# Turning a graph network's row tiles for TensorE: identity products and ScalarE copies, or transposing transfers

## The chip, the core and the metric

The kernel runs on one core of one Trainium2 chip. A core has a matrix engine (TensorE, in the profile PE, with its weight loads as PEld), VectorE (DVE), ScalarE (ACT), GpSimd (POOL) and SyncE (SP), which run side by side and meet at semaphores, and 16 DMA engines that move data between memories. ScalarE and SyncE each have a queue on which they issue transfers. The metric is the time of one execution on the device in microseconds (us); less is better.

## The reference

A graph with 1,250 nodes, 512 features and 21,250 directed edges goes through four residual layers, each followed by a layer norm over the features:

```python
x = layernorm(x + gcn(x))      # normalised adjacency, batch norm over nodes, gelu
x = layernorm(x + sage(x))     # two layers relu(h @ W_self + mean(h[src]) @ W_neigh + b)
x = layernorm(x + rgcn(x))     # two relations; w[r] = sum_b att[r,b] * basis[b], a sigmoid gate per node
x = layernorm(x + gin(x))      # relu((h + sum(h[src])) @ W1 + b1) @ W2 + b2
```

Each layer is made of products of the node matrix (1,250 x 512) with 512x512 weights, and of sums over a node's edges, which the kernel does as products with a dense count matrix.

## The kernel before

The nodes are ten tiles of 128 rows (`NT = 10`). After a first stage that counts the edges into `A` and `AT` and mixes the first basis matrices, the work goes through seven units, `UNITS`, numbered 0 to 6, with 1, 2, 2, 3, 3, 1 and 1 weight matrices. A unit has two phases:

- **dense**: for each tile `t`, `dense(t, j)` multiplies the tile of the input with each weight matrix. Numbers are kept as a sum of two float16 parts (high and low), so a product of a tile and a matrix is 12 matmuls of 128x128 by 128x512 (line 635). The bank pair is `j = t % 2`. ScalarE then takes the high part of the result out of PSUM (`z_out`, line 911), VectorE the low part (`z_low`, line 1265) and, where a unit has one, the node's own term (line 1273). `dense(t)` waits until that is done for tile `t - 2`.
- **aggregation**: for each tile, `agg(t, j)` sums over the neighbours (line 669, 20 matmuls per tile, 40 with two relations). VectorE and ScalarE turn the sum into the next unit's input: `after_agg` (line 1325), `ln_step` or `relu_step` for the high part in `S16`, `low_part` (lines 1280 and 1283) for the low one, which raises `s_ready`. Unit 0 aggregates in turned form (line 694), followed by the batch norm and `back` (line 704), and unit 6 has only the dense phase (`last_tile`, line 1352).

TensorE contracts over partitions, so a tile of `S16` (128 nodes x 1,024: high and low part) has to be turned before `dense(t)`. Before the change `turn(t, j)` does that: eight products of a 128x128 block with the identity `ident` into the PSUM tile `T` (line 609), and then ScalarE copies `T` into `hT[:, j]` in `hT_out` (line 855). `T` exists once and `hT` twice, so a tile is turned while TensorE works on the one before it, and `hT_out(t)` waits by `s_d` until `dense(t - 2)` is done.

Each engine runs its own list in the order in which the code is written. Beside the units run preparations: `PREP` and `SCALES` say after which tile ScalarE loads and splits the weights of a later unit (lines 792, 803, 806) and VectorE finds their largest value (line 1150), and `HALVES` says how many halves of a basis matrix VectorE adds into `acc` after each tile (line 1196, four instructions a half); SyncE loads those into `stage` (line 446) as `acc` is done with a quarter.

Of the kernel before, what the change touches and what calls it, by code (L numbers as in the profile page):

```python
# [7 lines left out]
REL, BASES = 2, 30  # L8
# [40 lines left out]
def resnorm_gnn_kernel(nc, x, src_t, dst_t, typ_t, dst_r, W0, b0, gamma, beta,  # L49
# [11 lines left out]
    with ctx:  # L61
# [181 lines left out]
        s_t = sem("s_t")  # L243
        s_hT = sem("s_hT")
# [148 lines left out]
        def sums_in(j, m):  # L393

            return max(n for n in range(NT) if SUM_BANK[n] == (j, m)) + 1

# [132 lines left out]
        def _(pe):  # L529
# [70 lines left out]
            for u, unit in enumerate(UNITS):  # L600
                nm, nz = len(unit["mats"]), unit["nz"]

                def turn(t, j, u=u):

                    pe.wait_ge(s_ready, NT * u + t + 1)
                    wait(pe, s_hT, t + NT * u)
                    for h in range(2):
                        for k in range(KT):
                            last = nc.tensor.matmul(T[:, h, k * P:(k + 1) * P],  # L609
                                                    S16[:, ds(t, 1), h * D + k * P:h * D + (k + 1) * P]  # L610
                                                    .rearrange("p a c -> p (a c)"), ident[:, :], start=True, stop=True)
                    last.then_inc(s_t, 1)

                def dense(t, j):
                    if nm == 1 and t < NT - 1:
                        turn(t + 1, 1 - j)
                    pe.wait_ge(s_hT, t + (NT * u + 1))
# [9 lines left out]
                    for m in range(nm):  # L627
# [5 lines left out]
                        for hp, wp in ((0, 0), (1, 0), (0, 1)):  # L633
                            for k in range(KT):
                                last = nc.tensor.matmul(Dp[:, j, m, :], hT[:, j, hp, k * P:(k + 1) * P],  # L635
                                                        weights_of(u, m)[:, wp, k, :], start=(n == 0), stop=(n == 3 * KT - 1))
# [3 lines left out]
                        if nm > 1 and m == 0 and t < NT - 1:  # L640
                            turn(t + 1, 1 - j)
# [14 lines left out]
                def agg(t, j):  # L656
# [3 lines left out]
                    if u and isinstance(t, int) and t == NT - 2:  # L660
                        turn(0, 0, u + 1)
# [50 lines left out]
                if u < 2:  # L712
                    turn(0, 0)
                for t in range(NT):
                    dense(t, t % 2)
                if u == 0:
                    pe.wait_ge(s_hT, NT)
# [16 lines left out]
        def _(act):  # L734
# [26 lines left out]
            def tile_out(t):  # L761
                for i in range(PER):
# [8 lines left out]
                    if i % 2 and 0 <= first < NT:  # L771
                        split_x(first)

            def split_x(t):
# [4 lines left out]
                nc.scalar.activation(S16[:, t, 0:D], w1[:, t % 2, :], ACT.Copy).then_inc(x_hi, 1)  # L779

# [68 lines left out]
            for u, unit in enumerate(UNITS):  # L849
                nz = unit["nz"]  # L850

                def hT_out(t, j, u=u):
                    act.wait_ge(s_t, t + (NT * u + 1))
                    wait(act, s_d, t + (NT * u - 1))
                    nc.scalar.activation(hT[:, j, :, :], T[:, :, :], ACT.Copy).then_inc(s_hT, 1)  # L855

# [66 lines left out]
                if u == 0:  # L923
                    hT_out(0, 0)
# [17 lines left out]
                def relu_step(t, j):  # L942
                    if t == NT - 2:
                        hT_out(0, 0, u + 1)
                    if t == NT - 1 and u in (1, 3):
                        hT_out(1, 1, u + 1)
# [39 lines left out]
                else:  # L986
# [17 lines left out]
                    for t in range(NT):  # L1004
                        deviation(t, t % 2)
                        if t == 1:
                            hT_out(0, 0, 1)
# [3 lines left out]
                        if t in turned_after and t != 1:  # L1011
                            hT_out(turned_after[t], turned_after[t] % 2, 1)
                        if t == 2:
                            hT_out(1, 1, 1)
# [474 lines left out]
```

## Time and profile before

| | |
|---|---|
| time, median of 3 runs (lowest to highest) | 980.29 us (979.81 to 981.43) |
| the profiled execution: its time, and its span in the trace | 977.63 us, 975.8 us |
| busy: PE, PEld, DVE, ACT, POOL | 95%, 48%, 69%, 36%, 9% |
| chain that ended last: PE, DVE, ACT, DMA | 73%, 16%, 3%, 3% |
| mean granted TensorE clock | 0.987 of full speed |

The span runs from the first instruction to the last. A busy share is an average over stages; which engine sets the pace differs from stage to stage. The chain is followed back from the last instruction to what released it each time, so what is not on it had time to spare.

### The profile page before, as it was taken

How to read it: one execution, taken by the hardware profiler on the slowest of the kernel's cores; microseconds unless marked ns; L12 is line 12 of the kernel's file. 1: busy time of each engine (PE TensorE's matmuls, PEld its weight loads, DVE VectorE, ACT ScalarE, POOL GpSimd, SP SyncE). 2: the span in 40 equal slices, each digit the busy share in tenths (PEclk: the TensorE clock that was granted, in tenths of full speed). 3: DMA queues.
4: the chain of work that ended last, by engine and by line, in shares of the span. 5: the costliest groups of instructions: out<-in, count | busy, mean ns of one | idle time of the engine just before them, and what ended most of it. 6: DMA issues, size and time to landing. Idle time of an engine off the chain costs nothing.

```text
span 975.8 us, 14273 instructions
## 1 busy us (share of the span) xinstructions
PE 928.6 (95%) x4880; PEld 465.1 (48%) x4880; DVE 677.9 (69%) x1469; ACT 348.0 (36%) x501; POOL 85.3 (9%) x66
## 2 busy tenths in 40 slices
PE   6899999989997999988998999999999999999997
PEld 2455555545555544443444444444444444454453
DVE  6698898843438679999999999996324234442358
ACT  0132444636864423433332322114422221143342
POOL 1000011210111002201211000001300010010000
PEclk9899999999998999999999999999999999999999
DMA  8755555523111165574532355540010013100015
GB/s 275 253 164 149 177 165 172 158 82 98 44 44 55 51 203 156 187 251 146 176 116 87 120 150 173 142 129 1 22 44 1 1 54 108 65 22 1 1 55 159
DMA packets 59456, 108.69 MB, mean 111 GB/s; under 512 B 6497, under 2 KB 6966, under 8 KB 59386
## 3 DMA queue, kind: packets, MB, share of 16 engines
q1 hardware_dynamic: 38522, 68.45, 22.8%
q10 hardware_dynamic: 20864, 39.33, 12.5%
q8 instruction: 41, 0.67, 0.3%
q14 instruction: 29, 0.24, 0.1%
HBM read 95.24 MB, written 12.52 MB: 110 GB/s over the span
## 4 chain that ended last, share of the span: by engine, by line
PE 73%; DVE 16%; ACT 3%; issue 3%; DMA 3%; DVEq 1%; POOL 1%; SPq 0%; ACTq 0%
PE Dp L635 28%; PE Dp L669 22%; PE T L579 9%; PE Dp L535 5%; DVE acc L1196 5%; PE Dp L694 4%; PE T L609 2%; PE Dp L704 1%; DVE stt L1288 1%; DVE w L1325 1%; DVE mcol L1150 1%; DMA Zraw<-in_basis 1%; DVE Zraw L1089 1%; DVE Zraw L1307 1%; DVE acc L1352 1%
## 5 line engine op out<-in xcount | busy, mean ns | idle before, releaser
L635 PE MATMUL Dp<-W,hT 128*128 128x512 f16 x1320 | 297.5, 381 | 4.5 <-ACT hT L855 3.6
L635 PEld LDWEIGHTS Dp<-W,hT 128*128 128x128 f16 x1320 | 127.5, 98 | 149.7 <-issue 5.4
L669 PE MATMUL Dp<-Zraw,A 128*128 128x512 f16 x800 | 173.3, 379 | 0.0
L1196 DVE SCALAR_TENSOR_TENSOR acc<-stage,att,acc 128x512 f32<-128x512 f32 x232 | 168.2, 793 | 0.2 <-DMA stage<-in_basis 0.2
L669 PE MATMUL Dp<-Zraw,AT 128*128 128x512 f16 x600 | 130.5, 379 | 0.0
L669 PEld LDWEIGHTS Dp<-Zraw,A 128*128 128x128 f16 x800 | 78.2, 98 | 93.9
L1089 DVE TENSOR_SCALAR Zraw<-hT,w 128x640 f16<-128x640 f16 (+1 forms) x240 | 110.6, 461 | 0.1
L855 ACT ACTIVATE hT<-T 128x1024 f16<-128x1024 f32 x70 | 71.4, 1020 | 84.9 <-PE T L609 78.3
L669 PEld LDWEIGHTS Dp<-Zraw,AT 128*128 128x128 f16 x600 | 58.6, 98 | 70.0
L1087 DVE TENSOR_SCALAR Zraw<-hT,w 128x128 f16<-128x128 f16 (+1 forms) x240 | 66.3, 276 | 26.4 <-PE Dp L535 17.3
L535 PE MATMUL Dp<-Zraw 128*128 128x320 f16 (+1 forms) x480 | 74.2, 301 | 1.7 <-DVE Zraw L1089 1.0
L1325 DVE SCALAR_TENSOR_TENSOR w<-Dp,aggc,S 128x512 f32<-128x512 f32 x40 | 29.9, 746 | 64.7 <-PE Dp L669 58.7
L1265 DVE SCALAR_TENSOR_TENSOR Zraw<-Dp,zsc,Zraw 128x512 f16<-128x512 f32 x30 | 22.5, 750 | 71.2 <-ACT Zraw L911 71.1
L579 PE MATMUL T<-stage,W 128*128 128x512 f32 x120 | 62.5, 642 | 9.9 <-DVE W L1050 8.5
L535 PEld LDWEIGHTS Dp<-Zraw 128*128 128x128 f16 (+1 forms) x480 | 46.6, 98 | 43.4 <-issue 26.3
L742 ACT ACTIVATE Zraw<-Dp 128x640 f16<-128x640 f32 x40 | 28.1, 703 | 106.3 <-PE Dp L535 106.3
L635 PE MATMUL Dp<-Zraw,hT 128*128 128x512 f16 x240 | 55.7, 387 | 8.7 <-ACT hT L855 6.2
L579 PE MATMUL T<-Zraw,W 128*128 128x512 f32 x120 | 58.5, 610 | 5.7 <-DMA Zraw<-in_basis 4.1
L911 ACT ACTIVATE Zraw<-Dp,zsc 128x512 f16<-128x512 f32 x50 | 32.2, 685 | 88.6 <-PE Dp L635 87.8
L952 ACT ACTIVATE w<-w,s_in 128x512 f32<-128x512 f32 x30 | 21.6, 720 | 118.1 <-DVE w L1325 118.1
L492 POOL TENSOR_TENSOR W<-wst,W 128x1024 f16<-128x1024 f32 x18 | 41.2, 2310 | 167.3 <-ACT W L806 167.3
L609 PEld LDWEIGHTS T<-ident,S 128*128 128x128 f16 x560 | 37.3, 99 | 21.7 <-issue 7.0
(162 smaller groups left out, 850.6 us busy)
## 6 DMA issues: line engine op xcount, KB each, us to landing
stage<-in_basis SPq DMA_DIRECT2D x180, 256.0 KB, 2.8
Zraw<-in_basis SPq DMA_DIRECT2D x60, 256.0 KB, 3.0
xres<-w ACTq DMA_DIRECT2D x30, 256.0 KB, 2.1
xr<-xres ACTq DMA_DIRECT2D x30, 256.0 KB, 2.7
wst<-in_Wn ACTq DMA_DIRECT2D x4, 1024.0 KB, 5.4
wst<-in_Ws ACTq DMA_DIRECT2D x4, 1024.0 KB, 5.2
wst<-mixd ACTq DMA_DIRECT2D x4, 1024.0 KB, 5.4
wst<-in_root ACTq DMA_DIRECT2D x3, 1024.0 KB, 5.8
```

The lines of the kernel that those rows point to most:

```text
L492: pool.tensor_tensor(weights_of(u, m)[:, 1, 2 * h:2 * h + 2, :], source, weights_of(u, m)[:, 0, 2 * h:2 * h + 2, :], ALU.subtract).then_in ...
L535: last = nc.tensor.matmul(Dp[:, j, b, 0:HALF], oh_lo[:, ds(slot * (2 * P) + q * P, P)], oh_key[:, ds(slot * (2 * KEYS) + (q * KEYS + b * H ...
L579: nc.tensor.matmul(T[:, 1, :], mixT[:, b * P:(b + 1) * P], mix_in[n % MIX_SLOTS], start=(b == 0), stop=(b == PAIRS - 1)).then_inc(s_mx, 1)
L609: last = nc.tensor.matmul(T[:, h, k * P:(k + 1) * P], S16[:, ds(t, 1), h * D + k * P:h * D + (k + 1) * P] .rearrange("p a c -> p (a c)"), ...
L635: last = nc.tensor.matmul(Dp[:, j, m, :], hT[:, j, hp, k * P:(k + 1) * P], weights_of(u, m)[:, wp, k, :], start=(n == 0), stop=(n == 3 * K ...
L669: last = nc.tensor.matmul(sum_bank(t), a[:, k, ds(t * P, P)], Z[:, r, h, k, :], start=(n == 0), stop=(n == count - 1))
L694: last = nc.tensor.matmul(Df[:, j, c:c + w], Z[:, 0, h, k, b * P:(b + 1) * P], AT[:, k, c:c + w], start=(k == 0 and h == 0), stop=(k == NT ...
L855: nc.scalar.activation(hT[:, j, :, :], T[:, :, :], ACT.Copy).then_inc(s_hT, 1)
L1087: v.tensor_scalar(oh_lo[:, ds(slot * (2 * P) + q * P, P)], iota_n[:, 0:P], lo_f[:, ds(c + q, 1)], None, ALU.is_equal)
L1089: last = v.tensor_scalar(oh_key[:, ds(slot * (2 * KEYS) + q * KEYS, KEYS)], iota_n, wkey[:, w:w + 1], key_f[:, ds(c + q, 1)], ALU.add, ALU ...
L1196: last = v.scalar_tensor_tensor(part, stage[:, q, :], a, part, ALU.mult, ALU.add)
L1325: v.scalar_tensor_tensor(w1[:, j:j + 1, :], sum_bank(t).rearrange("p (a d) -> p a d", a=1), c, rest, ALU.mult, ALU.add).then_inc(s_pre[u], 1)
```

## The change

`turn` and `hT_out` are gone. In their place ScalarE issues one transposing transfer per tile, from `S16[:, t, :]` to a turned tile of 128x8x128 (`turn_to`). There are four places for a turned tile in each unit except unit 1, which has two and two more for its tiles 6 and 7: the two of `hT` and two in a buffer that is idle in that unit (`w1`, the far end of `Zraw`, `wst`, `stage`), each with a semaphore of its own. Within the dense phase the transfer of tile `t + 3` is issued ahead of `z_out(t)`, and tiles 0 to 3 of a unit in the aggregation before it. The PSUM tile `T` stays for the first stage.

```diff
+        HT_RING = {0: ["w1a", "w1b", "a", "b"], 2: ["a", "b", "fara", "farb"], 3: ["a", "b", "wsta", "wstb"],
+                   4: ["a", "b", "stga", "stgb"], 5: ["a", "b", "stga", "stgb"], 6: ["a", "b", "stga", "stgb"]}
+        HT_NAMES = {(u, t): HT_RING[u][t % 4] if u != 1 else {6: "fara", 7: "farb"}.get(t, "ab"[t % 2])
+                    for u in range(NU) for t in range(NT)}
...
-                def turn(t, j, u=u):
-
-                    pe.wait_ge(s_ready, NT * u + t + 1)
-                    wait(pe, s_hT, t + NT * u)
-                    for h in range(2):
-                        for k in range(KT):
-                            last = nc.tensor.matmul(T[:, h, k * P:(k + 1) * P],
-                                                    S16[:, ds(t, 1), h * D + k * P:h * D + (k + 1) * P]
-                                                    .rearrange("p a c -> p (a c)"), ident[:, :], start=True, stop=True)
-                    last.then_inc(s_t, 1)
-
                 def dense(t, j):
-                    if nm == 1 and t < NT - 1:
-                        turn(t + 1, 1 - j)
-                    pe.wait_ge(s_hT, t + (NT * u + 1))
+                    turned = HT_SLOT[HT_NAMES[u, t]]
+                    pe.wait_ge(s_hT[HT_NAMES[u, t]], 16 * (len(hT_before(u, t)) + 1))
...
+            def turn_to(end, u):
+
+                for t in range(turned[u], min(end, NT)):
+                    slot = HT_NAMES[u, t]
+                    act.wait_ge(s_ready, NT * u + t + 1)
+                    for before, tile in hT_before(u, t)[-1:]:
+                        act.wait_ge(s_d, NT * before + tile + 1)
+                    if slot[:2] == "w1" and t < 2:
+                        act.wait_ge(s_ready, NT)
+                    elif slot[:3] == "far" and u == 1:
+                        act.wait_ge(s_tb, NT)
+                    elif slot[:3] == "wst" and t < 4:
+                        act.wait_ge(s_wlo, halves_split(3))
+                    elif slot[:3] == "stg" and u == 4 and t < 4:
+                        act.wait_ge(st_free[t - 2], BASES)
+                    act.dma_start_transpose(HT_SLOT[slot].rearrange("p h (k n) -> p (h k) n", k=KT),
+                                            S16[:, t, :]).then_inc(s_hT[slot], 16)
+                turned[u] = max(turned[u], min(end, NT))
...
-                def hT_out(t, j, u=u):
-                    act.wait_ge(s_t, t + (NT * u + 1))
-                    wait(act, s_d, t + (NT * u - 1))
-                    nc.scalar.activation(hT[:, j, :, :], T[:, :, :], ACT.Copy).then_inc(s_hT, 1)
...
                 def ln_step(t, j):
-                    if t == NT - 2 and u == 4:
-                        hT_out(0, 0, u + 1)
-                    if t == NT - 1:
-                        hT_out(1, 1, u + 1)
                     deviation(t, j)
-                    if t == NT - 3 and u == 2:
-                        hT_out(0, 0, u + 1)
+                    if t > 2:
+                        turn_to(min(t - 2, 4), u + 1)
...
                 def z_out(t, j):
-                    if not (t == NT - 1 or t == 0 and u in (2, 3, 4, 5) or u == 1 and t < 5):
-                        hT_out(t + 1, 1 - j)
+                    if t:
+                        turn_to(t + 4, u)
```

`relu_step` gets the same `turn_to(min(t - 2, 4), u + 1)` as `ln_step`, and the step over the tiles of the batch norm issues unit 1's first tiles where it copied them before. Tiles 0 and 1 of unit 0 are issued in the first stage, before its last window, and 2 and 3 at the start of unit 0.

What TensorE has in its list from unit 4's aggregation (line 669, two relations) into unit 5's dense phase (one weight matrix). Before, unit 5's first tile is turned inside the aggregation and an identity turn stands ahead of each further tile:

```order
L669 MATMUL Dp<-Zraw,A 128x512 x320
L609 MATMUL T<-ident,S 128x128 x8
L669 MATMUL Dp<-Zraw,A 128x512 x80
L609 MATMUL T<-ident,S 128x128 x8
L635 MATMUL Dp<-W,hT 128x512 x12
```

After (the product is line 639 there), two tiles are read from `hT`, the next two from `stage`, and so on:

```order
L669 MATMUL Dp<-Zraw,A 128x512 x400
L639 MATMUL Dp<-W,hT 128x512 x24
L639 MATMUL Dp<-W,stage 128x512 x24
L639 MATMUL Dp<-W,hT 128x512 x24
L639 MATMUL Dp<-W,stage 128x512 x24
```

Each 24 are two tiles of 12, and the eight identity products ahead of each tile are gone.

What ScalarE has in the batch norm's step over the tiles, which makes unit 1's input (line 863, in the changed kernel 878, takes the square root of the variance; 869, changed 884, writes the high part of the tile). Before, from tile 0's high part on:

```order
L869 ACTIVATE S<-w 128x512
L870 DMA xres<-w 128x512
L863 ACTIVATE sd<-mvr,epsc 128x1
L855 ACTIVATE hT<-T 128x1024
L869 ACTIVATE S<-w 128x512
```

After:

```order
L884 ACTIVATE S<-w 128x512
L885 DMA xres<-w 128x512
L878 ACTIVATE sd<-mvr,epsc 128x1
L797 DMA_TRANSPOSE hT<-S 128x8x128
L884 ACTIVATE S<-w 128x512
```

The transfer of tile 0 stands where its copy stood, behind tile 1's square root: it is not issued any earlier in the list than the copy was.

## Rows read from the trace of the kernel before

**Rows 1.** The page: busy time by engine, and the chain's shares by engine.

```profile
PE 928.6 (95%) x4880; PEld 465.1 (48%) x4880; DVE 677.9 (69%) x1469; ACT 348.0 (36%) x501; POOL 85.3 (9%) x66
...
PE 73%; DVE 16%; ACT 3%; issue 3%; DMA 3%; DVEq 1%; POOL 1%; SPq 0%; ACTq 0%
```

**Rows 2.** Windows: stretch, length, busy time of each engine (instructions), clock, DMA share.

```profile
209.80:249.00 39.20, 35.60 (x250) 20.38 (x251) 14.59 (x30) 21.04 (x30) 0.38 (x1) 0.96 0.31 97
...
413.00:480.00 67.00, 58.28 (x313) 27.70 (x313) 65.63 (x99) 26.98 (x33) 10.97 (x5) 0.97 0.57 186
480.00:523.80 43.80, 43.80 (x209) 19.91 (x207) 41.48 (x84) 10.93 (x19) 4.79 (x2) 1.00 0.41 128
523.80:609.70 85.90, 83.45 (x434) 39.69 (x434) 82.07 (x137) 25.55 (x36) 3.19 (x2) 0.98 0.45 136
...
865.00:894.90 29.90, 29.90 (x194) 15.68 (x193) 10.34 (x17) 14.52 (x20) 0.00 (x0) 1.00 0.03 9
```

**Rows 3.** Timeline of PE, units 4 and 5: start, duration, what.

```profile
707.27 0.61 PE L609 MATMUL T<-ident,S 128*128 128x128 f16 x8
707.72 7.93 PE L635 MATMUL Dp<-W,hT 128*128 128x512 f16 x36
...
868.45 2.75 PE L635 MATMUL Dp<-W,hT 128*128 128x512 f16 x12
871.04 0.61 PE L609 MATMUL T<-ident,S 128*128 128x128 f16 x8
871.49 2.75 PE L635 MATMUL Dp<-W,hT 128*128 128x512 f16 x12
```

**Rows 4.** The page's group of the copies; PE's waits from 209 us on.

```profile
L855 ACT ACTIVATE hT<-T 128x1024 f16<-128x1024 f32 x70 | 71.4, 1020 | 84.9 <-PE T L609 78.3
```

```profile
PE Dp L635 <- ACT hT L855: 9.8, 5, 3.2
```

**Rows 5.** Timeline, start of unit 0.

```profile
209.82 0.61 PE L609 MATMUL T<-ident,S 128*128 128x128 f16 x8 [0.73 <-issue]
...
213.47 1.01 PE L609 MATMUL T<-ident,S 128*128 128x128 f16 x8 [3.05 <-ACT hT L855]
...
214.28 3.68 PE L635 MATMUL Dp<-W,hT 128*128 128x512 f16 x12
```

**Rows 6.** Timeline, unit 1's tile 0: its low part, its first product.

```profile
303.79 0.66 DVE L1280 SCALAR_TENSOR_TENSOR S<-w,S 128x512 f16<-128x512 f32 x1
...
306.63 2.76 PE L635 MATMUL Dp<-W,hT 128*128 128x512 f16 x12 [1.12 <-ACT hT L855]
```

**Rows 7.** Window of DVE alone; then PE's timeline at unit 3's start.

```profile
365.00:541.00 176.00, 170.26 (x280) 0.98 0.49 158
```

```profile
526.27 4.45 PE L635 MATMUL Dp<-W,hT 128*128 128x512 f16 x12 [2.45 <-ACT hT L855]
```

**Rows 8.** Timeline of DVE: the own term of unit 3's tile 0.

```profile
543.40 0.74 DVE L1273 SCALAR_TENSOR_TENSOR S<-Dp,ownc,bias 128x512 f32<-128x512 f32 x1
```

**Rows 9.** Timeline, unit 6: VectorE's first step of tiles 1, 8 and 9.

```profile
945.11 0.75 DVE L1352 SCALAR_TENSOR_TENSOR acc<-Dp,ownc,bias 128x512 f32<-128x512 f32 x1 [0.95 <-PE Dp L635]
...
966.37 0.75 DVE L1352 SCALAR_TENSOR_TENSOR acc<-Dp,ownc,bias 128x512 f32<-128x512 f32 x1
...
969.35 0.75 DVE L1352 SCALAR_TENSOR_TENSOR acc<-Dp,ownc,bias 128x512 f32<-128x512 f32 x1
```

**Rows 10.** DMA issues, us to landing; issue time of line 858 (ns min/median/max).

```profile
xr<-xres ACTq DMA_DIRECT2D x30, 256.0 KB, 2.7
wst<-in_Wn ACTq DMA_DIRECT2D x4, 1024.0 KB, 5.4
...
b0T<-in_b SPq DMA_DIRECT2D x1, 2.0 KB, 8.8
```

```profile
L858 ACTq DMA_DIRECT2D xr<-xres x30: 326/326/462, 423.7 to 965.8; - x30
```

**Rows 11.** Timeline of ACT, unit 5: the high part of tile 2.

```profile
874.28 0.60 ACT L911 ACTIVATE Zraw<-Dp 128x512 f16<-128x512 f32 x1 [1.52 <-PE Dp L635]
```

More of the change, by code:

```diff
@@ L242, in resnorm_gnn_kernel @@
         s_wlo = sem("s_wlo")
-        s_t = sem("s_t")
-        s_hT = sem("s_hT")
+        s_hT = {n: sem(f"s_hT_{n}") for n in ("a", "b", "w1a", "w1b", "fara", "farb", "wsta", "wstb", "stga", "stgb")}
         s_d = sem("s_d")
@@ L395, in sums_in, with halves_view, hT_before @@
             return max(n for n in range(NT) if SUM_BANK[n] == (j, m)) + 1
+        def halves_view(flat):
+            return flat.rearrange("p (h d) -> p h d", h=2)
+        far = Zraw[:, 4 * NT * D - 4 * D:]
+        HT_SLOT = {"a": hT[:, 0], "b": hT[:, 1], "fara": halves_view(far[:, 0:2 * D]), "farb": halves_view(far[:, 2 * D:])}
+        for n, buffer in (("w1", w1), ("wst", wst), ("stg", stage)):
+            for i, side in enumerate("ab"):
+                HT_SLOT[n + side] = halves_view(buffer[:, i, :].bitcast(f16))
+        HT_RING = {0: ["w1a", "w1b", "a", "b"], 2: ["a", "b", "fara", "farb"], 3: ["a", "b", "wsta", "wstb"],
+                   4: ["a", "b", "stga", "stgb"], 5: ["a", "b", "stga", "stgb"], 6: ["a", "b", "stga", "stgb"]}
+        HT_NAMES = {(u, t): HT_RING[u][t % 4] if u != 1 else {6: "fara", 7: "farb"}.get(t, "ab"[t % 2])
+                    for u in range(NU) for t in range(NT)}
+        def hT_before(u, t):
+            return [a for a in HT_NAMES if a < (u, t) and HT_NAMES[a] == HT_NAMES[u, t]]
         BACK = {(0, 0): 4, (0, 1): 5, (1, 0): 6, (2, 0): 7, (2, 1): 8, (3, 0): 9}
@@ L634, in dense @@
                             for k in range(KT):
-                                last = nc.tensor.matmul(Dp[:, j, m, :], hT[:, j, hp, k * P:(k + 1) * P],
+                                last = nc.tensor.matmul(Dp[:, j, m, :], turned[:, hp, k * P:(k + 1) * P],
                                                         weights_of(u, m)[:, wp, k, :], start=(n == 0), stop=(n == 3 * KT - 1))
@@ L639, in dense @@
                             last.then_inc(s_d, 1)
-                        if nm > 1 and m == 0 and t < NT - 1:
-                            turn(t + 1, 1 - j)
                         if u == 1 and (t, m) in BACK:
@@ L659, in agg @@
                         pe.wait_ge(s_own[u], NT - 1 + SUM_BANK[t][0])
-                    if u and isinstance(t, int) and t == NT - 2:
-                        turn(0, 0, u + 1)
                     rels = [(A[:, r], r) for r in range(REL)] if nz == 2 else [(AT, 0)]
@@ L711, in _ @@
                         back(t)
-                if u < 2:
-                    turn(0, 0)
                 for t in range(NT):
@@ L772, in tile_out @@
                         split_x(first)
+                    if w == NWIN - 2:
+                        turn_to(2, 0)
             def split_x(t):
@@ L779, in split_x @@
                 nc.scalar.activation(S16[:, t, 0:D], w1[:, t % 2, :], ACT.Copy).then_inc(x_hi, 1)
+            turned = [0] * NU
+            def turn_to(end, u):
[15 more added lines that the diff above has]
+                turned[u] = max(turned[u], min(end, NT))
             loads, read = [0], {}
@@ L923, in _ @@
                 if u == 0:
-                    hT_out(0, 0)
+                    turn_to(4, 0)
                 def first_z(t, j):
@@ L942, in relu_step @@
                 def relu_step(t, j):
[L943 to L946, printed above, removed]
+                    if t > 2:
+                        turn_to(min(t - 2, 4), u + 1)
                     act.wait_ge(s_pre[u], t + 1)
@@ L1011, in _ @@
                         if t in turned_after and t != 1:
[L1012 removed]
+                            turn_to(turned_after[t] + 1, 1)
                         if t == 2:
[L1014 removed]
+                            turn_to(2, 1)
         @block.vector
```

3 lines of the change are left out of this document (1 added, 2 removed).

## The prediction

> **What bounds the kernel now.** I read the shares first: TensorE is busy for 95% of the span and has 73% of the chain that ended last, VectorE has 16% [rows 1]. That says where to look, not what a saved microsecond is worth, so I cut the span into the phases of the units with the windows. In unit 5's dense phase TensorE is busy for all of 29.90 us and VectorE for 10.34; from 413 to 480 and on to 524 us VectorE is busy for 98% and 95%, and in unit 3's dense phase for 82.07 of 85.90 us, beside a TensorE at 83.45 [rows 2]. So there are two kinds of stage: TensorE's own (units 0, 4, 5, most of 1, the later part of 3) and VectorE's (from about 365 us until unit 3's second tile).
>
> **What is removed.** 70 turns of eight identity products and 70 copies. A turn moves the products behind it by 0.45 us: it begins at 707.27 and the next products at 707.72; in unit 5 the turn at 871.04 is followed at 871.49, and a tile takes 3.04 us, of which 2.59 are products [rows 3]. (The 0.61 and 2.75 printed are pipelined and overlap.) If every turn were paid in time, 70 x 0.445 = 31 us would come back. The copies take 71.4 us of ScalarE, which has room, and their latency makes TensorE wait 9.8 us in five places ahead of products [rows 4].
>
> **What is added.** 70 transfers of 256 KB on ScalarE's queue. The trace has no transposing transfer, so both its prices are bounded. *Issue* (ScalarE is held by it): not under the 0.33 us of an ordinary 256 KB issue [rows 10]; above, I know of no row, and take twice the copy, 2.0 us. I choose 1.0, the copy's own length, as the work is cut into more pieces than in a plain issue, so ScalarE's occupation stays as it is. *Landing*: not under the 2.7 us of a plain 256 KB load; the nearest rows above are 5.4 us for 1 MB and 8.8 us for a transfer of only 2 KB in runs of a few bytes [rows 10]. A turned tile is also written in shorter runs than it is read, but it is a tile of 256 KB with full rows at its source, so I stay near the first row: 3.5 us from the beginning of the issue, the added part of the issue included. A gain in landing below 2.7 is excluded, as no row has it. The Trainium skill (Advanced Engine Details and Errata, X-Bar Transpose (TRN2)) says that transposing transfers on this chip are about as fast as plain ones, 350 to 400 GB/s. By it the landing would stay at the plain row's, and my sum would gain about 1 us. The same skill has a number that speaks against the change (VectorE: DVE Perf Modes, The three transpose paths): 1309 ns for a 128x128 block by DMA against 390 by TensorE. If that were the pace for each of the eight blocks, a tile would take 10.5 us and, by that estimate, the kernel would be over 15% slower; no row here shows which of the two holds.
>
> **The sum, stage by stage** (minus is a gain).
>
> Unit 0. Its first product starts at 214.28, after a turn at 209.82, the copy, and a second turn that waited 3.05 us, and it runs at about half the clock for part of its 3.68 us, against the 2.75 of [rows 3]; TensorE had just stood still [rows 5]. With tiles 0 and 1 turned during the last windows the product can start at the first turn's place: 4.5 + 0.9 us. Eight more turns, tiles 2 to 9, are 3.5. Against it: tiles 2 and 3 are now issued ahead of the scaling of the first result, 2 x 1.0 us on ScalarE, which dense(2) waits for, and tile 4 stands in the queue behind a 1 MB weight load of 5.4 us [rows 10]; I take 2.9 for both. **-6.0**.
>
> Unit 1, tile 0. Its low part ends at 303.79 + 0.66 = 304.45 and its product begins at 306.63 [rows 6]. The transfer can't be issued before 304.45, so the product is at 308.0: +1.4; and TensorE will have stood for nearly 3 us, as it had before the slow products of [rows 5] (another start after 2.45 us took 4.45 us for what elsewhere takes 2.75 [rows 3, 7]): +1.1. **+2.5**. This is the place where the cover is gone.
>
> Unit 1, tiles 1 to 9. Eight turns ahead of 365 us are 3.5; with two places only, tile t + 2 is issued when the products of t are done and has one tile's products, 5.2 us, to land, from which I take 1.5 for late issues behind the batch norm's chain. **-2.0**.
>
> 365 to 541 us. VectorE is busy 170.26 of 176 us [rows 7]. The some 23 turns here, and TensorE's waits at 413 to 527 us, are in the shadow of VectorE; of its own 5.7 idle us about one was spent on late products. **-1.0**. TensorE will just wait longer, on VectorE's own terms.
>
> Unit 3. dense(2) needs the own term of tile 0, which VectorE ends at 543.40 + 0.66 = 544.06 [rows 8], and TensorE gets there at 544.4: from 526.27, 4.29 for the slow first twelve, a turn and 5.18 for the rest of tile 0, a turn and 7.77 for tile 1 [rows 3, 7]. From there the pace is TensorE's: 7.93 printed, 8.22 with the turn, 7.77 without, and VectorE's work per tile is below that (82.07 us with ten tiles and the tail of unit 2 in the stretch). Seven turns remain: **-3.1**.
>
> Aggregation of 3, unit 4, aggregation of 4, unit 5, aggregation of 5: 1 + 9 + 1 + 9 + 1 turns, each in a list with no gap: **-9.3**. ScalarE's round in unit 5 is 0.60 for the high part (it idled 1.52 before it [rows 11]), 0.2 of latency and now 1.0 for an issue, under 2.59.
>
> Unit 6. The last two tiles of VectorE are 969.35 - 966.37 = 2.98 us apart, while TensorE delivers one in 3.04; tile 1 waited 0.95 for it [rows 9]. So VectorE takes over: about 1.0 at tile 1 and 0.05 a tile after: **-1.3**.
>
> Sum: -6.0 + 2.5 - 2.0 - 1.0 - 3.1 - 9.3 - 1.3 = -20.2 us. The profiled execution took 977.63 (span 975.8 and 1.8 around it), which becomes 957.4; the median of the runs stands 2.7 above that execution, so I predict **960 us**. With the low bounds (0.33 issue, 2.7 landing) units 0 and 1 give 6 us more: 954.
>
> **Rivals.** (1) *ScalarE is held longer by the issues*: 2.0 us each. In unit 5 its round is 2.0 + 0.2 + 0.6 = 2.8 us for the six tiles issued there, so a tile saves 0.24, not 0.45 (1.2 less); in unit 0, where loads and evictions stand in the same list, 4 of the 6 us go; unit 1 loses 1 or 2 more: 967. For: ScalarE has much in unit 0. Against: in all other stages it idles. (2) *The other sign: the transfers follow one another at a price c, and TensorE waits for each.* In a unit with one matrix tile 4 is issued after the first products; the phase takes 2.6 + 6c + 2.6 us against 30.4. At c = 5.4, 37.6: +7.2 in unit 5, +7 in unit 6, in unit 0 with eight transfers 8 x 5.4 + 2.6 = 45.8 against 39.2 [rows 2], +6.5; unit 1 with its two places +6 and its start +4; the 10 us elsewhere stay: 21 slower, 1001. At 8.8 it is 28 + 27 + 34 + 33 + 8 - 10 = 120, 1100. It decides from c = 4.7 on. For: the short runs' 8.8 us. Against: 2.7 us for the same bytes, and DMA engines busy for 0.03 in unit 5 [rows 2]. Its other way in, loads of `stage` made late for VectorE, has slack: in unit 3 a quarter is used again after a tile, 7.8 us, and 256 KB land in 2.7. The skill's 1309 ns, from the section named above, are this rival at c = 10.5; by the slope between my two points, 29 us for each us, that estimate is 1150, and I give what lies above 1100 a chance of 0.06. (3) *Nothing comes of it*: VectorE's stretch also swallows unit 0's and unit 1's gains and a landing near 4.5 us the rest: 980. For: between 413 and 524 us VectorE has 3.7 us of idle time in all [rows 2], so that nothing gained or lost before shows there. Against: what lies after 544 us, 13.7 us of the sum, doesn't go through VectorE.
>
> **How the numbers follow.** My forecast (948 to 964) has 0.50, rival 1 and its like (964 to 978) 0.22, rival 3 0.04, rival 2 0.24, half of it below 1001. 0.2% is about what a measurement tells from no change. Faster 0.72, same 0.04, slower 0.24. The range 948 to 1001 leaves out about 0.12 above and 0.03 below, and is so wide since the price of landing is unknown.
>
> **What would show it.** Line 639's products in unit 5 every 2.59 us; unit 4's tile in 7.77; the first product of unit 0 near 209.8; unit 1's first product 3 us and more behind its low part, at less than full clock; VectorE still busy without a gap where it was; transfers that land in 3 to 4 us. I am wrong if TensorE waits inside dense phases for a turned tile, above all in units 5 and 6, or if ScalarE's issues are long enough to make the high parts late.

## The result and the profile after

The changed kernel takes **965.5 us** (965.4 to 966.5, four runs) beside 980.05 us for the kernel before in the same series (978.3 to 981.4, four runs): a ratio of 0.9855, with a 95% interval from 0.9837 to 0.9872. That is 14.5 us faster; 960 was predicted, with a range from 948 to 1001. The profiled execution has a span of 963.5 us where the one before had 975.8, so the spans differ by 12.3 us, against the 20.2 of the sum. Two executions of a kernel below (the late half) took 2255 and 3311 us, far outside all others, and its figures leave them out.

The page of the changed kernel, busy time by engine and the chain by engine, answers to [rows 1]:

```profile
PE 903.1 (94%) x4320; PEld 435.0 (45%) x4320; DVE 679.1 (70%) x1469; ACT 280.7 (29%) x431; POOL 84.7 (9%) x66
...
PE 67%; DVE 21%; DMA 4%; issue 3%; ACT 2%; DVEq 1%; ACTq 1%; POOL 1%; SPq 0%
```

560 products and 70 ScalarE operations are gone. TensorE has lost 6 points of the chain and VectorE has gained 5, so the next thing to look for is in VectorE's stages.

The two prices that the prediction had to bound, the issue and the landing of a transfer (the changed kernel's view of one tile; count, duration in ns as minimum, median and maximum, first and last start, and further down in the same answer the time from issue to landing):

```profile
L797 ACTq DMA_TRANSPOSE hT<-S x42: 1246/1250/4042, 211.5 to 945.0; - x42
...
DMA to landing us min/median/max: 3.1/3.2/13.3
```

So an issue holds ScalarE's queue for 1.25 us (1.0 taken), and a tile lands 3.2 us after its issue began (3.5 taken). Both lie inside the bounds and near the value taken. The Trainium skill (VectorE: DVE Perf Modes, The three transpose paths) has 1309 ns for one 128x128 block; taken as a pace for eight blocks it gives an estimate of 10.5 us. This trace shows that it is no pace: the eight land together in 3.2.

Where TensorE waits ahead of unit products now (the waits of the changed kernel: sum in us, times, longest); it answers to the second fence of [rows 4]:

```profile
PE Dp L639 <- DVE S L1282: 18.8, 5, 6.4
PE Dp L639 <- DVE Zraw L1274: 3.7, 2, 3.1
...
PE Dp L639 <- DMA hT<-S: 3.3, 1, 3.3
...
DVE acc L1205 <- DMA stage<-in_basis: 2.3, 3, 1.0
```

One product waits for a transfer in the whole program, at unit 1's tile 0. The 18.8 us are VectorE's own terms in its stretch, as forecast (3.5 us before the change). The last line was 0.2 us before: VectorE now waits for quarters of the basis in `stage`.

To see where the time went I cut both traces at the same seven points: the first product or turn of unit 0 (F), the first product of unit 1 (U1), the start of aggregation 1 (A1), VectorE's own term of unit 3's tile 0 (S, [rows 8]), the starts of aggregations 3 and 5 (A3, A5), and the end. Each number is a difference of two starts in the timelines:

| us | F to U1 | U1 to A1 | A1 to S | S to A3 | A3 to A5 | A5 to end |
|---|---|---|---|---|---|---|
| before | 96.8 | 62.6 | 174.1 | 66.3 | 285.2 | 80.9 |
| after | 92.9 | 60.1 | 178.6 | 65.7 | 277.1 | 78.8 |
| difference | -3.9 | -2.6 | +4.5 | -0.6 | -8.1 | -2.1 |

They sum to -12.8; the stage ahead of F is 0.5 us longer in the execution after. The chain of gains breaks in two places: the 6.4 us gained before A1 shrink to 2.0 by S, and from S to A3, where 3.1 were forecast, 0.6 came.

The rows that stand at those places in the changed kernel: unit 0's third tile and unit 1's first, which answer to [rows 5] and [rows 6], unit 3's third tile, and unit 5's dense phase, which answers to [rows 3] (start, duration, what, in brackets the idle time before and who ended it):

```profile
210.29 2.75 PE L639 MATMUL Dp<-W,w 128*128 128x512 f16 x12 [0.73 <-issue]
...
219.62 4.44 PE L639 MATMUL Dp<-W,hT 128*128 128x512 f16 x12 [3.08 <-DVE Zraw L1274]
...
303.23 5.30 PE L639 MATMUL Dp<-W,hT 128*128 128x512 f16 x12 [3.30 <-DMA hT<-S]
...
542.81 18.31 PE L639 MATMUL Dp<-W,wst 128*128 128x512 f16 x72 [6.41 <-DVE S L1282]
...
863.94 5.34 PE L639 MATMUL Dp<-W,stage 128*128 128x512 f16 x24 [0.65 <-DVE Zraw L1274]
869.12 5.34 PE L639 MATMUL Dp<-W,hT 128*128 128x512 f16 x24
874.29 5.34 PE L639 MATMUL Dp<-W,stage 128*128 128x512 f16 x24
```

The reader is to see two things. In unit 5 two tiles start 5.18 us apart, 2.59 each, with no turn between them. And where TensorE has stood for some 3 us or more in this execution, what follows is slow: twelve products in 4.44 and in 5.30 us instead of 2.75, and 72 in 18.31 where two tiles of [rows 3]'s kind take 2 x 7.77 = 15.5. The weight loads of that last row, one ahead of each product, show why (timeline of the weight loads, changed kernel):

```profile
543.19 0.15 PEld L639 LDWEIGHTS Dp<-W,wst 128*128 128x128 f16 x1 [0.28 <-issue]
543.62 0.15 PEld L639 LDWEIGHTS Dp<-W,wst 128*128 128x128 f16 x1 [0.28 <-issue]
544.05 0.15 PEld L639 LDWEIGHTS Dp<-W,wst 128*128 128x128 f16 x1 [0.28 <-issue]
```

They are 0.43 us apart for the first dozen, and 0.216 at full clock (2.59 / 12). The granted clock from 542.80 to 548.00 is 0.50: the engine runs at 1.2 GHz, the lower of its two levels.

### The profile page after: what moved, and what is told of

Its sections match the earlier page's. It is cut to its first block, busy times and chain, and to the rows that moved or that the text cites. A ratio compares the mean times of both kernels' runs of the same rounds, so it can differ in the third digit from the quotient of the medians.

```text
span 963.5 us, 13083 instructions
## 1 busy us (share of the span) xinstructions
PE 903.1 (94%) x4320; PEld 435.0 (45%) x4320; DVE 679.1 (70%) x1469; ACT 280.7 (29%) x431; POOL 84.7 (9%) x66
## 2 busy tenths in 40 slices
DMA packets 133371, 126.97 MB, mean 132 GB/s; under 512 B 80417, under 2 KB 80886, under 8 KB 133306
## 4 chain that ended last, share of the span: by engine, by line
PE 67%; DVE 21%; DMA 4%; issue 3%; ACT 2%; DVEq 1%; ACTq 1%; POOL 1%; SPq 0%
PE Dp L669 24%; PE Dp L639 22%; PE T L595 9%; DVE acc L1205 6%; PE Dp L551 5%; PE Dp L694 4%; DVE stt L1297 2%; DVE mcol L1159 1%; DVE w L1334 1%; DVE Zraw L1274 1%; DVE S L1282 1%; DVE Zraw L1316 1%; DMA stage<-in_basis 1%; DMA Zraw<-in_basis 1%; DVE w L1356 1%
## 5 line engine op out<-in xcount | busy, mean ns | idle before, releaser
L639 PE MATMUL Dp<-W,hT 128*128 128x512 f16 x816 | 184.3, 385 | 6.8 <-DMA hT<-S 3.3
L639 PEld LDWEIGHTS Dp<-W,hT 128*128 128x128 f16 x816 | 80.4, 99 | 104.5 <-issue 9.3
L639 PE MATMUL Dp<-W,stage 128*128 128x512 f16 x240 | 52.8, 379 | 0.6 <-DVE Zraw L1274 0.6
L694 PE MATMUL Dp<-AT,Zraw 128*128 128x512 f16 (+1 forms) x240 | 43.4, 344 | 0.0
L639 PE MATMUL Dp<-Zraw,hT 128*128 128x512 f16 x144 | 34.6, 401 | 6.1 <-DVE S L1282 6.1
```

What stands on the lines that cost most here:

```text
L639: last = nc.tensor.matmul(Dp[:, j, m, :], turned[:, hp, k * P:(k + 1) * P], weights_of(u, m)[:, wp, k, :], start=(n == 0), stop=(n == 3 * ...
L694: last = nc.tensor.matmul(Df[:, j, c:c + w], Z[:, 0, h, k, b * P:(b + 1) * P], AT[:, k, c:c + w], start=(k == 0 and h == 0), stop=(k == NT ...
```

## The experiments

Two theories on the first gap. *Shadow*: VectorE is busy nearly all the time from A1 to S, so whatever is gained before A1 is swallowed, whatever is done. *Crowding and clock*: the transfers themselves cost something there (late basis quarters, a late first tile with a slow product behind it), and the gains would carry if they did not. On the second gap: the low clock behind the 6.4 us wait, or VectorE's own work.

**Spare products ahead of unit 3's third tile.** They keep TensorE busy while it waits, and nothing reads their result.

```
+        KEEP = {(3, 2): 24}
...
+                    for _ in range(KEEP.get((u, t), 0)):
+                        nc.tensor.matmul(T[:, 0, :], ident[:, :], A[:, 0, 0, 0:D], start=True, stop=True)
```

> The changed kernel with 24 spare products (identity by a piece of A, into the PSUM tile T that nothing else uses by then) ahead of unit 3's tile 2, where TensorE stands still for 6.4 us for VectorE's own terms. My theory: that standing costs 2.6 us afterwards, as the first twelve products of tile 2 run at the lower clock (0.43 us apart, against 0.22) and TensorE sets the pace from there on. So the products of tile 2 should run at full clock and the kernel should take 2.0 to 2.6 us less than the changed kernel, some 963 us. Rival: VectorE sets the pace of unit 3's dense phase (7.27 us a tile against 7.77), or the spare products make tile 2 late, and the time stays at 965.5 within 0.7 us.

Measured: 963.8 us, ratio 0.9839 (0.9824 to 0.9853). The timeline of TensorE:

```profile
534.14 5.34 PE L622 MATMUL T<-A,ident 128*128 128x512 f16 x24
540.70 15.70 PE L642 MATMUL Dp<-W,wst 128*128 128x512 f16 x72 [1.23 <-DVE S L1285]
```

The same 72 products now take 15.70 us instead of 18.31, and the stretch from S to A3 takes 63.0 us instead of 65.7. So the low clock cost 2.6 us there. The whole time moved by less than its interval is wide, and the stretch is what shows it.

**Unit 1's tile 0 turned by TensorE** as in the kernel before, all other tiles by transfers.

```
+        ON_PE = sorted({(1, 0)})
...
+                    if by_pe(u, t):
+                        pe.wait_ge(s_copied, ON_PE.index((u, t)) + 1)
```

A turn is again eight identity products and a copy by ScalarE; `by_pe` says for which tiles, and the experiments below that name `ON_PE` differ in that set alone.

> The changed kernel, but tile 0 of unit 1 is turned by eight identity products and a ScalarE copy, as before the change; all other tiles by transfers. In the changed kernel that tile makes TensorE wait 3.3 us for the transfer and then costs 2.6 us at the lower clock, 3.4 us more than before the change. My theory: an early gain is carried through VectorE's stretch, so the kernel takes 2.5 to 3.4 us less than the changed one, some 962.5 us. Rival: what is gained ahead of 365 us is swallowed between 365 and 543 us by VectorE's waits, and 0 to 1 us comes back, 964.5 to 965.5 us.

Measured: 962.0 us, ratio 0.9813 (0.9788 to 0.9837), 3.5 below the change. Tile 0's product and the wait for the basis in this kernel's trace:

```profile
301.52 2.76 PE L662 MATMUL Dp<-W,hT 128*128 128x512 f16 x12 [1.12 <-ACT hT L846]
```

```profile
DVE acc L1268 <- DMA stage<-in_basis: 6.8, 5, 2.4
```

The product is at full clock again, and A1 comes 148.9 us after F instead of 153.0. But S comes 330.9 after F, as against 331.6: in this execution, which took 2.1 us more than the median of its kernel, the 4.1 us are nearly all gone again, with 6.8 us of waits for basis quarters instead of 2.3.

**Unit 2 turned by TensorE**, all other tiles by transfers.

```
+        ON_PE = sorted({(u, t) for u in (2,) for t in range(NT)})
```

> The changed kernel, but the ten tiles of unit 2 are turned by identity products and copies; the other units by transfers. It asks where 4 us of the gain went between 365 and 543 us. My theory: the transfers of unit 2 crowd the DMA queues (they take 8.1 us to land there, DMA share 0.78 against 0.58 before) and make three loads of the basis matrices late for VectorE (2.3 us of waits), and GpSimd's work falls on VectorE's at another place. TensorE has the time for the turns there. I expect VectorE's waits for those loads to be gone and the kernel 1.5 to 3 us faster than the changed one, 963 us. Rival: the loss is only where GpSimd's splitting of weights falls, by chance; then the time stays within 1 us of 965.5.

Measured: 962.7 us, ratio 0.9829 (0.9815 to 0.9843), 2.8 below the change, though ten turns and copies came back. F to S takes 327.4 us instead of 331.6. Of these 4.2 us only 1.6 are idle time of VectorE; the other 2.6 are a shorter busy time (255.6 us for 258.2), to which the last part of this document comes back. How long a quarter of the basis takes to land between 400 and 480 us, in the changed kernel and then in this one (the DMA issues of that window, KB each, median us to landing):

```profile
stage<-in_basis SPq DMA_DIRECT2D x33, 256.0 KB, 3.7
hT<-S ACTq DMA_TRANSPOSE x4, 8.1
```

```profile
stage<-in_basis SPq DMA_DIRECT2D x34, 256.0 KB, 3.0
```

In the kernel before it was 2.9. The traces of the other kernels agree: 3.2 to 4.0 us where unit 2 goes by transposing transfers, 2.7 to 3.0 where it does not. So these transfers make the quarters of the other queue later there, by 0.7 to 0.8 us in this pair, and take 8.1 us themselves. That this is what makes the kernel faster is not shown by it, as the larger part of the 4.2 us is VectorE's busy time.

**Plain transfers in place of transposing ones** (the tiles arrive unturned, so the products are of other numbers).

```
-                    act.dma_start_transpose(HT_SLOT[slot].rearrange("p h (k n) -> p (h k) n", k=KT),
-                                            S16[:, t, :]).then_inc(s_hT[slot], 16)
+                    act.dma_start(HT_SLOT[slot].rearrange("p h (k n) -> p (h k) n", k=KT),
+                                  S16[:, t, :].rearrange("p (k n) -> p k n", k=2 * KT)).then_inc(s_hT[slot], 16)
```

> The changed kernel with plain transfers of the same 256 KB from the same tile to the same place instead of transposing ones, so the tiles are not turned and the result is another. It measures what the turning in the transfer costs: my theory is that a plain issue holds ScalarE 0.33 us instead of 1.25 and lands in 2.3 to 2.7 us instead of 3.2 with a DMA share back near 0.6 in unit 2, so that unit 1 starts 1.4 us earlier, unit 0 about 1 us, and VectorE's late loads go: 961 to 963 us. Rival: it is the bytes, not the turning, that crowd the queues, and the time stays within 1 us of 965.5.

Measured: 961.5 us, ratio 0.9805 (0.9785 to 0.9824), 4.0 below the change. Issue and landing of these transfers:

```profile
L797 ACTq DMA_DIRECT2D hT<-S x42: 472/472/721, 210.4 to 942.7; - x42
...
DMA to landing us min/median/max: 2.3/2.4/8.0
```

That is the price of transposing in itself: 0.78 us more of issue, 0.8 us more of landing, and in all some 4 us of the kernel. Basis quarters land in 2.8 us in the window above and VectorE waits for none. The packets differ with it: 133371 in the changed kernel, of which 80417 are under 512 B, and 69531 here for the same 127.0 MB. Yet F to S takes 330.3 us, only 1.3 less than with transposing, so in this execution (1.6 us above the median of its kernel) late quarters are a small part of what is lost before S.

**The halves.** Transfers only in units 0 to 2 (units 3 to 6 turned by TensorE), and the reverse.

```
+        ON_PE = sorted({(u, t) for u in (3, 4, 5, 6) for t in range(NT)})
```

> Units 3 to 6 turned as before (eight identity products a tile and ScalarE's copy), units 0 to 2 by transfers as in the change. Theory (VectorE's stretch between 365 and 541 us swallows what units 0 and 1 gain): TensorE reaches unit 1's aggregation 5 to 6 us earlier, but the second unit-3 tile's successor begins only about 1.5 us earlier than in the kernel before, and from there each tile costs 0.45 us more than in the change: 977 to 978.5 us. Rival (the early gains carry to the end): about 975. If early transfers cost on the whole: 980 or more.

Measured: 975.2 us, ratio 0.9957 (0.9941 to 0.9973), 4.4 below the kernel before.

```
+        ON_PE = sorted({(u, t) for u in (0, 1, 2) for t in range(NT)})
```

> Units 0 to 2 turned as before, units 3 to 6 by transfers. Theory (nearly all of the gain lies behind unit 3's second tile, and the transfers of units 1 and 2 cost VectorE's stretch some late loads of its basis quarters): 980.0 less 10.2 measured behind agg 3's start and 1 to 3 in unit 3, so 966.5 to 969 us, hardly slower than the change's 965.5. Rival (the gains of units 0 and 1 carry to the end): 971 or more. The two kernels' gains should add up to about the 14.5 us of the change if the halves are independent; more if the transfers in units 0 to 2 cost something that the later ones then lose.

Measured: 969.9 us (968.7 to 973.1, four executions), ratio 0.9906 (0.9883 to 0.9930), 9.8 below the kernel before by the medians and 9.2 by the ratio. The early half came out on the rival's side: 975 is what was worked out for early gains that carry to the end. The late half lies between its theory (966.5 to 969) and the rival (971 or more) and decides nothing by itself. The two gains sum to 14.2 us, and the change has 14.5; with intervals of 1.6 and 2.3 us on them that is additive within what can be told.

The traces of the two halves say more. In the early half's profiled execution F to S is 331.4 us, as in the change (331.6). In the late half's it should be near the 333.6 of the kernel before, as both turn units 0 to 2 by TensorE and only unit 3's first tiles differ ahead of S, and it is 336.0 (stretch, length, busy time of TensorE, weight loads, VectorE, ScalarE, GpSimd; kernel before, then late half):

```profile
209.82:543.40 333.58, 311.41 (x1702) 159.22 (x1703) 255.86 (x469) 148.97 (x206) 41.50 (x22) 0.97 0.38 123
```

```profile
210.11:546.06 335.95, 309.76 (x1682) 157.50 (x1682) 258.14 (x470) 147.06 (x205) 39.87 (x22) 0.98 0.40 125
```

Up to A1 the two take the same time (159.5 us); the 2.4 us come behind it, and 2.3 of them are VectorE's busy time. So a difference of 2.4 us in F to S can come about without any transfer in units 0 to 2, and the 2.0 us that the change gained by S in the table are a lower figure: against the late half's trace it gained 4.3, which is what the early half's times say (4.4). The kernel before was profiled in an execution that is 2.4 us below its median, the change in one at its median. The stage ahead of F differs between the profiled executions too, by up to 4.7 us (F from 208.3 to 213.0).

**Both repairs together**: unit 1's tile 0 and unit 2 by TensorE.

```
+        ON_PE = sorted({(1, 0)} | {(2, t) for t in range(NT)})
```

> Unit 1's tile 0 and all of unit 2 turned by TensorE, the rest by transfers. If the two repairs mend different things (the start of unit 1; the load on the DMA queues under VectorE's stretch), they add: 965.5 less 3.6 and 2.8, 959 us, and the wait for basis quarters stays under 2 us. Rival (both feed the same stretch of VectorE, which lets only one gain through): 961.5 to 963, as each alone.

Measured: 960.0 us, ratio 0.9789 (0.9767 to 0.9811). That is nearer to the two repairs added up (959) than to one alone (961.5 to 963), but the interval is 2.2 us to either side and reaches the latter's edge. The windows F to U1, U1 to A1, A1 to S, for the changed kernel and then for this one (length, then busy time and instructions of TensorE, weight loads, VectorE, ScalarE, GpSimd; clock; DMA share; GB/s):

```profile
210.29:303.23 92.94, 81.18 (x442) 44.92 (x443) 42.45 (x109) 54.06 (x74) 11.95 (x8) 0.94 0.34 92
303.23:363.30 60.07, 60.07 (x288) 30.47 (x289) 45.50 (x86) 12.28 (x24) 0.00 (x0) 0.95 0.66 161
363.30:541.92 178.62, 160.22 (x713) 70.35 (x711) 170.28 (x278) 52.27 (x77) 27.70 (x14) 0.96 0.65 175
```

```profile
211.18:302.61 91.43, 81.95 (x451) 45.72 (x451) 41.42 (x106) 54.17 (x74) 11.96 (x8) 0.94 0.33 91
302.61:359.76 57.15, 57.15 (x288) 29.31 (x289) 46.76 (x88) 12.98 (x26) 0.00 (x0) 1.00 0.69 171
359.76:535.75 175.99, 164.07 (x793) 74.90 (x791) 169.84 (x277) 61.98 (x87) 29.06 (x14) 0.97 0.52 162
```

F to S is 324.6 us: 7.0 less than in the change, 9.0 less than before. Read VectorE's column. Its busy time is the same in both, 258.2 and 258.0 us; what differs is its idle time, length less busy: 50.5 + 14.6 + 8.3 = 73.4 us in the change, 50.0 + 10.4 + 6.2 = 66.5 here. In the kernel before it is 54.8 + 16.3 + 6.6 = 77.7, with 255.9 busy. So the account that holds is that of VectorE from F on: it has some 256 to 258 us of work before S, done partly ahead of A1, and each microsecond in which it idles, early or late, is paid at S. That is an account of where the time went, not yet a reason why idle time comes back. *Shadow*, by which no gain before A1 can carry, falls: such a gain carries when it takes idle time from VectorE, and it is lost when more idle time comes back later. The waits for the basis between F and S are 0.6 us in this execution.

**The same with spare products**: 24 ahead of unit 3's third tile, 10 ahead of unit 0's.

```
+        KEEP = {(0, 2): 10, (3, 2): 24}
```

> The same, and spare products that keep TensorE's clock up: 24 ahead of unit 3's tile 2 and 10 ahead of unit 0's tile 2. If the low clock behind the wait is the cost there (half speed for a dozen products and more), it is 2 to 2.6 us faster than the kernel without them for unit 3 and up to 1.5 for unit 0, 956 to 959.5. Rival (the time is VectorE's there and the spare products only fill a wait): no difference.

Measured: **955.0 us**, ratio 0.9747 (0.9729 to 0.9765): 10.5 us faster than the change and the best of all kernels run. The timeline of TensorE at the two places:

```profile
219.09 2.32 PE L640 MATMUL T<-A,ident 128*128 128x512 f16 x10
221.86 2.75 PE L665 MATMUL Dp<-W,hT 128*128 128x512 f16 x12 [0.45 <-DVE Zraw L1340]
...
532.20 5.34 PE L640 MATMUL T<-A,ident 128*128 128x512 f16 x24
538.77 15.70 PE L665 MATMUL Dp<-W,wst 128*128 128x512 f16 x72 [1.23 <-DVE S L1348]
```

Full clock at both. Unit 3's brought what it had alone: S to A3 is 63.0 us against 65.9. Unit 0's made F to U1 2.0 us shorter (89.4 against 91.4), but F to S is 324.9 against 324.6, so nothing of it reached S in this execution: VectorE's idle time fell by 2.1 us before U1 and rose by 1.7 from U1 to A1. This profiled execution is the slowest of the kernel's five, 3.8 us above their median, so it doesn't tell what unit 0's spare products do in the others: of the 5.0 us between the medians of the last two kernels, unit 3's stretch has 2.9 and the rest has no place in the trace.

**How far ahead a transfer must be issued.** In units 5 and 6 alone, at the same place of ScalarE's list, tile t + 2, t + 1 or t is issued instead of t + 3.

```
-                        turn_to(t + 4, u)
+                        turn_to(t + (3 if u > 4 else 4), u)
```

> As the change, but in units 5 and 6 tile t + 2 is issued where tile t + 3 is (the first four tiles of each unit stay issued during the aggregation ahead of it). In the change's trace the issue of unit 5 starts right behind the high part of tile t - 1, so tile t + 2 has 2 x 2.59 = 5.2 us until its products; it lands in 3.2. Theory (landing 3.2 us, and only the landing counts): no wait, 965 to 967 us. Rival (transfers follow one another at a price near 4.7 us or more): unit 5 gets longer by 5 us or more.

Measured: 964.2 us, ratio 0.9846 (0.9813 to 0.9878), the change's own time. With 2 in place of 3:

> Tile t + 1 is issued there: it has 2.59 us to land in 3.2 and a little latency. Theory: every second tile of unit 5 waits 0.7 us, six tiles, about 2 us more; in unit 6 VectorE's 2.97 us a tile hide most of it: 967 to 969 us. Rival (a transfer costs more when the next follows closely, or less than the traces say): over 972, or no change.

Measured: 971.7 us, ratio 0.9908 (0.9877 to 0.9939). With 1:

> Tile t itself is issued there, when TensorE is about to need it: nothing covers the landing. Theory: unit 5 waits 3.3 us at each of six tiles, 20 us; in unit 6 the issue stands behind VectorE's statistics of two tiles before, 8 to 18 us: 993 to 1004 us, slower than the kernel before. If it stays near 966, landing costs nothing and the prediction's worry about it was empty; each stall should also bring TensorE's clock down, which would add up to 1.5 us a tile.

Measured: 1014.9 us, ratio 1.0375 (1.0340 to 1.0410). Unit 5 with tile t + 1, then with tile t (timeline of TensorE):

```profile
864.37 5.34 PE L639 MATMUL Dp<-W,stage 128*128 128x512 f16 x24 [0.64 <-DVE Zraw L1274]
870.36 5.35 PE L639 MATMUL Dp<-W,hT 128*128 128x512 f16 x24 [0.65 <-DMA hT<-S]
876.36 5.37 PE L639 MATMUL Dp<-W,stage 128*128 128x512 f16 x24 [0.65 <-DMA stage<-S]
```

```profile
871.34 2.76 PE L639 MATMUL Dp<-W,hT 128*128 128x512 f16 x12 [3.24 <-DMA hT<-S]
877.33 4.24 PE L639 MATMUL Dp<-W,hT 128*128 128x512 f16 x12 [3.23 <-DMA hT<-S]
```

Unit 5 does what a landing of 3.2 us says: every second tile waits 3.24 - 2.59 = 0.65 us when one tile covers it, every tile 3.23 us when none does. Two numbers of my expectations were too small. Unit 6 lost 4.0 us with one tile ahead (A5 to the end, 82.8 against 78.8), where I had expected most to be hidden: its issues stand behind VectorE's statistics on ScalarE's list, and two tiles waited 2.25 and 2.02 us for their transfers. And with no cover the eight tiles of unit 5 from the third on took 50.9 us against 20.7: 19.4 of the 30.2 are the six waits, and 9.9 are products behind five of them that took 4.24 to 5.30 us instead of 2.75, at the low clock. This is the prediction's second rival made on purpose, with its sign: transfers that TensorE waits for do make the kernel slower than before.

## Why the prediction was right, and where its terms were off

**The number was nearer than the sum.** The sum would have made the span 975.8 - 20.2 = 955.6 us, and it is 963.5: 7.9 us off. The 960 came closer to the median of 965.5 because 2.7 us were added for an execution of the kernel before that lay below its median, and the change was profiled at its own. That part was luck.

**The sign and the prices** were right: issue 1.25 us for 1.0, landing 3.2 for 3.5. Rival 1 didn't come: the 1.25 us and a high part of 0.60 fit into 2.59, and the issues run beside the high parts (one begins at 869.38, its high part at 869.32). Rival 2 needed a pace of 4.7 us per tile; the six transfers issued within unit 5 began between 862.29 and 874.56, the last four 2.59 us apart, and no product there waited for one. Rival 3 fell with what lies behind S.

**Aggregation 3 to the end**: -10.6 forecast (9.3 + 1.3), -10.2 measured from A3 on (8.1 + 2.1). Twenty turns of 0.445 us would be 8.9; unit 5 gives 0.65 back at its third tile, which now waits for VectorE's low part, a wait that a turn used to cover. In unit 6 VectorE took over at 2.97 us a tile, as forecast. This half of the sum is shown, by the segments and by the late half's trace (A3 to A5 277.1 there as well).

**Unit 0 and unit 1's tile 0**: the product of tile 0 in unit 1 was to come 6.0 - 1.4 = 4.6 us earlier, counted from F, and came 3.9. Unit 0's term was 1.1 us too large (its aggregation began 34.4 us after F for 39.3 before, so 4.9 earlier, not 6.0): its third tile stood 3.1 us for the low part and then ran at half clock, 1.7 us more. The loss at unit 1's tile 0 was forecast at 2.5 and was 3.6: 1.0 for the later start behind the low part, and 2.5 for the low clock behind the wait of 3.3 us, which held for all twelve products, 5.30 us for 2.76.

**Unit 1's tiles 1 to 9** were under-rated: U1 to A1 is 2.6 us shorter in spite of a first product 2.5 us longer, so the rest gave 5.1, not 2.0: nine turns, 4.0, and the 0.9 us for which TensorE had stood in that stretch (61.70 busy of 62.64 before, 60.07 of 60.07 after). Two places were enough.

**The step that failed is the sum across VectorE's stretch.** The prediction had S 6.5 us earlier after F (-6.0, +2.5, -2.0, -1.0); it came 2.0 earlier by the traces of the kernel before and the change, and 4.3 to 4.4 by the late half's trace and the early half's times. The step took lengths of TensorE's phases ahead of 365 us and carried them over a stretch that is VectorE's. What carries is VectorE's time: its idle time was 4.3 us less before U1, 1.7 less before A1 and 1.7 more from A1 to S, and its busy time rose by 2.4. The waits for basis quarters are 2.3 us in the change, 1.7 of them behind A1, and 0.2 before. The prediction had looked at that way in ("loads of `stage` made late for VectorE, has slack") and found slack in unit 3; in unit 2 there was none.

The 2.4 us of busy time are longer instructions, not more of them, and they are longer where they meet GpSimd's work on the weights (VectorE, then GpSimd, changed kernel):

```profile
446.81 2.73 DVE L1205 SCALAR_TENSOR_TENSOR acc<-stage,att,acc 128x512 f32<-128x512 f32 x4
...
463.57 6.48 DVE L1205 SCALAR_TENSOR_TENSOR acc<-stage,att,acc 128x512 f32<-128x512 f32 x4
```

```profile
464.00 4.84 POOL L508 TENSOR_TENSOR W<-wst,W 128x1024 f16<-128x1024 f32 x2 [20.91 <-ACT W L826]
```

The same four instructions take 2.73 us alone and 6.48 beside GpSimd, where two of the four take 2.6 us each instead of 0.74. The Trainium skill (Advanced Engine Details and Errata, GPSIMD Details) says that GpSimd shares a read and a write interface with VectorE and conflicts with its instructions of two SBUF inputs, which these are; this trace agrees, with 3.7 us for one such meeting. I compared each VectorE instruction between F and S with the median of its kind: in all ten traces cut so, every one that is over 0.1 us longer runs beside an instruction of GpSimd. Together they are 15.1 us too long in the kernel before, 14.9 with unit 2 turned by TensorE, 16.7 with unit 3's spare products alone, and 17.4 to 17.7 in the other seven. The late half is one of the seven (17.6, busy 258.1 us), though it turns units 0 to 2 as before, so the transfers of these units are not what makes the 2.4 us. I take them for the luck of which instructions meet; nothing here was run to move GpSimd's work.

**Unit 3**: -3.1 forecast, -0.6 measured from S to A3. The seven turns did go, but the wait for S, at which the turn of the next tile used to stand, became an unbroken 6.4 us, and the clock behind it took 2.6 back. The prediction had this mechanism at unit 1 and did not apply it here, though it wrote that TensorE will wait longer. Shown by the spare products, alone and in the best kernel.

**What stays open**: what decides which of VectorE's instructions meet GpSimd's, and with it 2.4 us of S; how much of the early half the late quarters cost; and how the 4 us that plain transfers save are spread, since their trace has 1.3 of them before S and none behind it.

## What to carry to other kernels

Where a second engine is the bound of a stretch, add up that engine's idle time from the last point where both were free, not the lengths of the first engine's phases: a gain that does not take idle time from it will not arrive. Where work is moved from an engine to transfers, ask of each place what covers the landing (here 3.2 us, so two tiles of 2.59), and leave the old way where nothing does; eleven of 70 tiles turned by TensorE after all were worth 5.5 us. Compare a stretch in more than two traces before calling 2 us in it a gain or a loss: here two kernels with the same turns in units 0 to 2 differ by 2.4. And TensorE can pay a second time behind a wait: filling one of 6.4 us with spare products shortened its stretch by 2.6 us, for one line.

## What the runs showed of the hardware

A transposing transfer of 256 KB within SBUF held ScalarE's queue for 1.25 us, a plain one of the same shape for 0.47, and an ordinary load for 0.33 [rows 10]. It landed in 3.2 us against 2.4. The Trainium skill (Advanced Engine Details and Errata, X-Bar Transpose (TRN2)) calls transposing transfers as fast as regular ones; by landing they are a third slower here, and by issue 2.6 times as dear. They come as many packets under 512 B (80417 in the changed kernel, 7617 with plain transfers), and beside them loads on the other queue landed in 3.7 us instead of 2.8 (medians from 400 to 480 us).

TensorE's clock: after 24 spare products and 1.23 us of standing still 72 products took 15.70 us, full clock. In the change each wait ahead of unit products of 3.08, 3.30, 4.96, 6.23 and 6.41 us was followed by products below full clock. But with transfers issued late, after a first wait of 3.24 us twelve products took 2.76 us, and the next, behind another 3.23 us, took 4.24; and behind 2.25 us 24 products took 7.04 us for 5.34, behind 2.02 us twelve took 2.76. So a wait of 2 to 3 us didn't cost the same each time, and these runs do not show what decides it.

VectorE beside GpSimd: a `scalar_tensor_tensor` of 128x512 float32 with two inputs in SBUF took 2.62 us for 0.74, while the one that reads one input from PSUM (`w<-Dp,aggc,S`, at 393.67 and 499.28 us in the change) took its 0.74 us beside GpSimd too.
